# Cross-attention and soft mixture of experts on one core: Mu's norms spread through memory, and the second layer norm's first part on GpSimd

## The reference

```
x = x + cross_attention(layernorm(x), ctx, pos)     # 32 heads of 8, rotary positions
z = layernorm(x); x_ln = layernorm(z) * gamma + beta
mu_n = mu / |mu|  over the 256 rows, for each of 16 experts x 128 slots
logits = normalised(x_ln) * scale @ mu_n
dispatch = softmax over the 64 rows; combine = softmax over the 2048 slots
out = combine @ (gelu((dispatch.T @ x_ln) @ W1 + b1) @ W2 + b2)
x = x + out
```

## Time and profile before

| | us |
|---|---|
| median of 3 runs (lowest, highest) | 476.96 (475.56, 477.92) |
| the profiled execution, its span | 477.61, 475.7 |
| PE busy, PEld busy | 444.3, 382.1 |
| DVE, ACT, POOL busy | 389.0, 286.7, 182.8 |
| start until T_0 | 23.4 |
| attention steps, T_0 to T_15 | 153.4 |
| the rest | 298.9 |

### The profile page before, as it was taken

How to read it: one execution, slowest core, us unless ns; L and a number is a source line. 1 busy time by engine, 2 the same in 40 slices (tenths; PEclk the granted TensorE clock), 3 DMA queues, 4 the chain that set the end, 5 groups by cost and what they waited for, 6 DMA issues and landing times.

```text
span 475.7 us, 12795 instructions
## 1 busy us (share of the span) xinstructions
PE 444.3 (93%) x4816; PEld 382.1 (80%) x4816; DVE 389.0 (82%) x857; ACT 286.7 (60%) x553; POOL 182.8 (38%) x322
## 2 busy tenths in 40 slices
PE   0679999999999999999999999999999999999996
PEld 0557787878887778878888988988988988988985
DVE  6689888898889877977977977977977877887775
ACT  3457777778888666365466466457457447447443
POOL 4479998379996332114112112112112112202100
PEclk9979999999999799999999999999999999999999
DMA  8930000000003000223213223312312312312330
GB/s 231 271 152 23 3 3 23 1 4 1 3 1 72 3 2 1 52 56 83 68 52 84 68 55 77 77 50 72 83 50 66 88 50 61 99 44 55 99 92 22
DMA packets 27815, 28.54 MB, mean 60 GB/s; under 512 B 10960, under 2 KB 19072, under 8 KB 27520
## 3 DMA queue, kind: packets, MB, share of 16 engines
q1 hardware_dynamic: 27392, 27.48, 22.1%
q10 hardware_dynamic: 384, 0.52, 0.5%
HBM read 9.11 MB, written 2.10 MB: 24 GB/s over the span
## 4 chain that ended last, share of the span: by engine, by line
PE 74%; DVE 14%; POOL 4%; SPq 3%; DMA 2%; issue 2%; ACT 1%; ACTq 0%; DVEq 0%; POOLq 0%
PE bank L1025 13%; PE bank L1027 12%; PE bank L1026 12%; PE bank L1241 10%; PE bank L1121 6%; PE bank L1263 6%; PE bank L1104 3%; PE bank L1085 3%; PE bank L1142 2%; SPq L293 2%; DVE kT L758 2%; DMA xa<-in_x 2%; DVE pT L904 2%; DVE on L777 1%; DVE pb L932 1%
## 5 line engine op out<-in xcount | busy, mean ns | idle before, releaser
L904 DVE STREAM_TRANSPOSE pT<-eb 128x512 f32<-128x512 f32 x64 | 44.5, 700 | 38.3 <-ACT eb L618 35.0
L1241 PE MATMUL bank<-w_raw,eb 128*128 128x130 f32 x512 | 60.8, 276 | 1.3 <-DVE w_raw L895 1.3
L1241 PEld LDWEIGHTS bank<-w_raw,eb 128*128 128x128 f32 x512 | 58.5, 190 | 2.7 <-DVE w_raw L895 2.3
L629 ACT ACTIVATE pb<-pb 128x768 f32<-128x768 f32 (+1 forms) x48 | 37.2, 774 | 28.2 <-DVE pb L932 28.2
L1025 PE MATMUL bank<-mun_h,xlT_l 128*128 128x512 f32 x128 | 52.1, 407 | 0.0
L932 DVE TENSOR_TENSOR pb<-bank,rh 128x384 f32<-128x384 f32 x96 | 49.3, 513 | 3.3
L624 ACT CAST xlT_h<-bank 128x256 fp32r<-128x256 f32 x16 | 5.9, 372 | 76.1 <-PE bank L1213 76.1
L618 ACT ACTIVATE eb<-bank,nshift,rn 128x512 f32<-128x512 f32 x64 | 46.2, 776 | 7.8 <-PE bank L1027 7.6
L1027 PE MATMUL bank<-mun_h,xlT_h 128*128 128x512 f32 x128 | 50.5, 395 | 0.0
L545 ACT COPY pT<-bank 128x512 f32<-128x512 f32 x64 | 37.6, 588 | 21.3 <-PE bank L1104 20.5
L1026 PE MATMUL bank<-mun_l,xlT_h 128*128 128x512 f32 x128 | 50.5, 394 | 0.0
(11 more groups left out here) (159 smaller groups left out, 1155.4 us busy)
## 6 DMA issues: line engine op xcount, KB each, us to landing
mu_raw<-pT SPq DMA_DIRECT2D x248, 64.0 KB, 2.0
mu_raw<-in_L_ffn_mu SPq DMA_DIRECT2D x1, 2048.0 KB, 10.1
out<-w_raw SPq DMA_DIRECT2D x16, 128.0 KB, 1.9
xa<-in_x SPq DMA_DIRECT2D x1, 1536.0 KB, 8.5
w_raw<-in_L_ffn_W SPq DMA_DIRECT2D x2, 512.0 KB, 10.1
w_raw<-in_L_ffn_W SPq DMA_DIRECT2D x1, 1024.0 KB, 7.3
xa<-in_x SPq DMA_DIRECT2D x1, 512.0 KB, 3.5
ctile<-in_ctx SPq DMA_DIRECT2D x1, 512.0 KB, 5.2
```

The source lines that it names most:

```text
L904: v.transpose(eblk[:, :, 4 * c:4 * c + 4, :].rearrange("p m e j -> p e m j"), eb[:, 4 * c:4 * c + 4, :].rearrange("p e (m j) -> p e m j", ...
L1241: m = mm(bank[HB[i]][:, n * 2 * HC:(n + 1) * 2 * HC], eb[:, e, :], xw[:, e, :], start=True, stop=True)
```

## The change

Mu's norms no longer go through PE and ScalarE. Behind its context loads SP writes the 2048 norms as one row into memory, waits until it has landed, and loads the row into all 128 partitions of `mu_rb`. GpSimd waits for that once and scales Mu in steps 9 to 12. The eight instructions of the moments of tiles 0 to 10 move from VectorE's step 12 to GpSimd, behind its step 14, with the deviations behind them (these were behind step 13). The two centres move from VectorE's step 13 to GpSimd, each ahead of its affine. VectorE gets a wait for the deviations ahead of its first `ffn_step`.

```diff
 sync:      load_ctx(2, 12, 16)
+           sp.wait_ge(mur_ready, 1)
+           sp.dma_start(norm_row.rearrange("(e s) -> s e", s=SLOTS), mu_r[:, 1, :], ...).then_inc(row_loaded, 16)
+           sp.wait_ge(row_loaded, 16)
+           sp.dma_start(mu_rb, row(norm_row, ES)).then_inc(rb_loaded, 16)
 gpsimd:
+           def moments(t0, t1):      # the eight instructions of VectorE's moments, with its waits
+               ...
+           def center(t):
+               g.tensor_scalar(xl[:, t, :], xa[:, t, :], ln2[:, 4, t].unsqueeze(1), ln2[:, 6, t].unsqueeze(1),
+                               ALU.subtract, ALU.mult).then_inc(z_ready, 1)
 scale_mu:
-               if k == 0:
-                   pool.wait_ge(rb_ready, c + 1)
+               if c == 0 and k == 0:
+                   pool.wait_ge(rb_loaded, 16)
             step(7, (mu_norms, ()))
+            step(8)
             for c in range(NQ):
-                step(8 + c, (scale_mu, (c, 0)), (scale_mu, (c, 1)))
-            step(12)
+                step(9 + c, (scale_mu, (c, 0)), (scale_mu, (c, 1)))
             step(13)
-            pool.wait_ge(var_ready, 1)
+            step(14)
+            pool.wait_ge(st2_ready, TILES - LATE)
+            moments(0, TILES - LATE)
+            pool.wait_ge(zvar_step, 8)
             deviations(ln2, 0, TILES - LATE, r2_step, 0, r2_ready)
-            step(14)
+            pool.wait_ge(r2_ready, 1)
...
+            center(0)
             affine(0, 0)
+            center(1)
             affine(1, 1)
 scalar:
-            def rb_copy(c):
...
 vector:
-                if s == TILES - 4:
-                    dve.wait_ge(st2_ready, TILES - LATE)
-                    moments(st2, ln2, 0, TILES - LATE, 1 + LN_EPS, LN_EPS * LN_EPS, var_step, 0, var_ready)
-                if s == TILES - 3:
-                    dve.wait_ge(r2_ready, 1)
-                    center(0, 0)
-                    center(1, 1)
...
+            dve.wait_ge(r2_ready, 1)
             ffn_step(0, 0, first=True)
 tensor:
-            def spread_norms(c):
...
-                if 8 <= s < 8 + NQ:
-                    spread_norms(s - 8)
...
-                if 8 <= s < 8 + NQ:
-                    pe.wait_ge(rb_ready, s - 7)
```

More of the change, by code:

```diff
@@ L148, in build @@
         mur_ready = sem("mur_ready")
-        rb_filled = sem("rb_filled")
-        rb_ready = sem("rb_ready")
+        row_loaded = sem("row_loaded")
+        rb_loaded = sem("rb_loaded")
         muscale_step = sem("muscale_step")
@@ L199, in build @@
         z_ready = sem("z_ready")
+        zvar_step = sem("zvar_step")
         aff_step = sem("aff_step")
@@ L240, in build @@
         out_d = out.rearrange("b s d -> (b s) d").rearrange("(t p) d -> p t d", p=P)
+        norm_row = nc.dram_tensor("norm_row", (ES,), F32, kind="Internal").ap()
         def row(v, n):
@@ L315, in _ @@
             load_ctx(2, 12, 16)
+            sp.wait_ge(mur_ready, 1)
+            sp.dma_start(norm_row.rearrange("(e s) -> s e", s=SLOTS), mu_r[:, 1, :], allow_slow_non_contiguous=True)                .then_inc(row_loaded, 16)
+            sp.wait_ge(row_loaded, 16)
+            sp.dma_start(mu_rb, row(norm_row, ES)).then_inc(rb_loaded, 16)
             sp.wait_ge(mu_ready, NQ * KD)
@@ L385, in deviations @@
                     .then_inc(done, 1)
+            def moments(t0, t1):
+                L = [ln2[:, i, t0:t1] for i in range(8)]
+                st = [st2[:, t0:t1, i] for i in range(6)]
+                g.tensor_tensor(L[0], st[1], st[4], ALU.add).then_inc(zvar_step, 1)
+                g.tensor_tensor(L[1], st[1], st[4], ALU.subtract).then_inc(zvar_step, 1)
+                g.tensor_tensor(L[2], st[2], st[5], ALU.add).then_inc(zvar_step, 1)
+                pool.wait_ge(zvar_step, 3)
+                g.tensor_scalar(L[4], L[0], 0.5, None, ALU.mult).then_inc(zvar_step, 1)
+                g.tensor_tensor(L[3], L[1], L[1], ALU.mult).then_inc(zvar_step, 1)
+                pool.wait_ge(zvar_step, 5)
+                g.tensor_scalar(L[3], L[3], DIM / 4.0, None, ALU.mult).then_inc(zvar_step, 1)
+                pool.wait_ge(zvar_step, 6)
+                g.tensor_tensor(L[2], L[2], L[3], ALU.add).then_inc(zvar_step, 1)
+                pool.wait_ge(zvar_step, 7)
+                g.tensor_scalar(L[5], L[2], (1 + LN_EPS) / DIM, LN_EPS * LN_EPS, ALU.mult, ALU.add)\
+                    .then_inc(zvar_step, 1)
+            def center(t):
+                g.tensor_scalar(xl[:, t, :], xa[:, t, :], ln2[:, 4, t].unsqueeze(1), ln2[:, 6, t].unsqueeze(1),
+                                ALU.subtract, ALU.mult).then_inc(z_ready, 1)
             def split_pool(raw, halves, base, done):
@@ L513, in _ @@
                 if t == 0:
-                    pool.wait_ge(var_ready, 2)
+                    pool.wait_ge(var_ready, 1)
                     deviations(ln2, TILES - LATE, TILES, r2_step, 5, r2_ready)
@@ L576, in xT_high, with step @@
                 a.copy(flat(xT[0][:, t % 2]), bank[7][:, 0:3 * P]).then_inc(xT_split, 1)
-            def rb_copy(c):
-                act.wait_ge(rb_filled, c + 1)
-                a.copy(mu_rb[:, c * BANK:(c + 1) * BANK], bank[6][:]).then_inc(rb_ready, 1)
-            def step(s, norms=None):
+            def step(s):
                 if s >= 1:
                     pT_copy(s - 1, 3)
-                if norms is not None:
-                    rb_copy(norms)
                 exp_group(s, 0)
@@ L663, in _ @@
             for s in range(TILES):
-                step(s, s - 8 if 8 <= s < 8 + NQ else None)
+                step(s)
             act.wait_ge(shift_ready, 1)
@@ L1004, in _ @@
             stats(TILES - 1)
+            dve.wait_ge(r2_ready, 1)
             ffn_step(0, 0, first=True)
             dve.wait_ge(st2_ready, TILES)
-            moments(st2, ln2, TILES - LATE, TILES, 1 + LN_EPS, LN_EPS * LN_EPS, var_step, 7, var_ready)
+            moments(st2, ln2, TILES - LATE, TILES, 1 + LN_EPS, LN_EPS * LN_EPS, var_step, 0, var_ready)
             ffn_step(1, 1)
```

## The result

The changed kernel takes 477.91 us (475.90 to 480.08 in 20 runs) against 476.62 (474.94 to 478.24 in 20 runs): ratio 1.0029, interval 1.0016 to 1.0041. It is slower by 0.16 to 0.41 percent, where 472.0 was forecast.

The account below looks back on a forecast made before the run. PE, holding 74% of the chain, was taken to set the time. Terms 2.77 + 3.54 - 0.86 - 0.13 = 5.32 gave 472.3 against the profiled 477.61, 471.6 against the median; forecast 472.0, range 470.6 to 475.2.

Parts of the forecast that it names:

- The row through memory: Norms written, then broadcast, before GpSimd's step 9: 5.4 + 6.4 = 11.8 us of 14.15 allowed, no cost.
- the estimate beside it, 10.1: Row write by the skill's rule at W1's price: 10.1 + 6.4 = 16.5, GpSimd 2.35 late, time 474.4.
- the row is late: Rival: both transfers cost 10.1, PE waits 5.1 us in step 10, half clock follows: 480.5; chance 0.07.
- Spreading by PE goes: Steps 8 to 11: without the spreading matmuls they become plain steps of 9.49 us, a gain of 2.77.
- Moments and centres leave VectorE: Step 13 becomes a plain step if the half clock goes with the stall: a gain of 3.54 us.
- `scale_mu` one step later: GpSimd falls 0.6 us behind per scaling step; PE waits 0.27 in step 12, 0.59 in step 13: costs 0.86.
- the half clock stays: Rival: PE's 0.59 us wait in step 13 keeps the half clock; price 2.5, time 474.5; chance 0.22.
- Moments, deviations and centres on GpSimd: Behind `rope_sums(15)`: tile 0 ready at T_14 + 11.32, so PE waits 0.13 us.
- GpSimd is slower at the moments: Rival: moments at upper bound, tile 0 comes 2.8 us later, PE waits in step 15: 474.8; chance 0.06.
- The sum: Whole change: 2.77 + 3.54 - 0.86 - 0.13 = 5.32 us gained.

Follow-up runs that it names:

- the wide row: Changed kernel with the norms turned by a PE transpose and VectorE copy, written as 16 pieces of 512 bytes: 472.44 us, ratio 0.9917.
- the write alone: Kernel before with the write of 2048 norms as 4-byte pieces added, read by nobody, PE and ScalarE still spreading: 481.18 us, ratio 1.0102.
- the moments alone: Kernel before with only moments and first two centres moved to GpSimd, norms still spread by PE: 474.44 us, ratio 0.9976.
- Lighter steps: Kernel of the wide row with Mu's eight halves scaled 2, 2, 1, 2, 1 in steps 9 to 13: 471.21 us, ratio 0.9909.
- the row by slots: Changed kernel with the row written as 128 pieces of 64 bytes, GpSimd reading with a 64-byte step: 475.90 us, ratio 0.9986.
- the quarter of the row: Kernel before with 512 pieces of 4 bytes written side by side, read by nobody: 483.79 us in one execution.

## Why the prediction was wrong

**The step that failed is "The row through memory".** It took the row's landing from the positions (5.4 us) and W1 (10.1), and concluded "no cost". The row took 10.7, over the upper bound. That alone would hardly have hurt. The broadcast landed 4.7 us after its issue (the page's issue list), so both took 15.4 us. The 14.15 allowed were too few, because `add_bout` also stands ahead of the first scaling. In the wide row that scaling starts 4.61 us behind T_9, not 3.96, so 14.8 were allowed and with plain steps the two would have been 0.6 late:

```profile
122.42 1.27 POOL L467 TENSOR_TENSOR mu_raw<-mu_raw,eb 128x512 f32<-128x512 f32 x1
```

What was wrong is the frame: the step asked only when the row arrives, and who waits for it. Nobody waited for it in step 9, but PE, ScalarE and VectorE stood still while it settled, and PE came back at half clock. That is 4.95 us, and that the write of the small pieces causes it is shown from both sides: the write alone brings it into the kernel before (14.51 us in step 8), and leaving it out, making it wide, setting the pieces apart or sending them to SBUF takes it away. Both bounds were loads into SBUF; neither could show how small pieces side by side settle in memory.

The rival "the row is late" had the right transfer but another mechanism: it put the loss at PE's wait for a late GpSimd, in step 10, and there is none there (9.50 us).

The rule of the Trainium skill that the prediction weighed ("DMA: Bandwidth & Descriptors", section "Rules for kernel authors" and the specifications: one descriptor for each element, read-modify-write below 512 bytes) pointed at the right transfer. That the estimate beside it, 10.1, was close to 10.7 is luck: it is the price of W1, a load of 64 times as many bytes. Nor does size alone decide: pieces of the same 4 bytes landed in 4.1 us when they were 64 bytes apart.

**Spreading by PE goes:** right. Steps 9 to 12 take 9.50 us; step 8 would, as the wide row shows (9.49).

**Moments and centres leave VectorE:** the mechanism was right, the size was not. Step 13 fell to a plain step (9.50 with the moments alone), but the 3.54 us rested on one execution whose half clock lasted long. In most traces the same stall costs 11.5 - 9.5 = 2.0 us, and the timed gain of this part alone is 1.5. The term was too large by some 1.5 us.

**`scale_mu` one step later:** right, and a little dear. GpSimd's `rope_sums` starts behind T by 1.38, 1.91, 2.47 and 3.07 us in steps 10 to 13, on its timeline after, with PE's wait in step 13 below:

```profile
133.87 1.64 POOL L386 TENSOR_TENSOR qkr<-ra,rb 128x256 f32<-128x256 f32 x2
...
143.90 1.66 POOL L386 TENSOR_TENSOR qkr<-ra,rb 128x256 f32<-128x256 f32 x2
...
153.96 1.67 POOL L386 TENSOR_TENSOR qkr<-ra,rb 128x256 f32<-128x256 f32 x2
...
164.06 1.64 POOL L386 TENSOR_TENSOR qkr<-ra,rb 128x256 f32<-128x256 f32 x2
...
165.75 0.33 PE L1089 MATMUL bank<-ident,qkr 128*128 128x128 f32 x1 [0.37 <-POOL qkr L386]
```

The step grows by 0.25. Behind the standstill GpSimd starts step 9 earlier, 0.84 us behind T_9; in the wide row it starts 1.11 behind, and PE waits 0.16 us in step 12 and 0.70 in step 13:

```profile
160.90 0.33 PE L1096 MATMUL bank<-ident,qkr 128*128 128x128 f32 x1 [0.70 <-POOL qkr L389]
```

That is the 0.86 of the forecast, but the two steps grow by only 0.61. Lighter steps take it away. The rival "the half clock stays" didn't come true at these waits: the clock is 1.00 in both steps. It did in the row by slots, behind a wait of 1.19.

**Moments, deviations and centres on GpSimd:** right. On GpSimd's timeline the eight moments take 173.43 to 175.59, 2.16 us (2.3 forecast), and the deviations 3.35 (3.34):

```profile
173.43 0.23 POOL L400 TENSOR_TENSOR ln<-st 128x11 f32<-128x11 f32 x1
...
175.59 2.14 POOL L360 TENSOR_TENSOR ln<-ln,mhalf 128x11 f32<-128x11 f32 x1
...
178.73 0.21 POOL L369 TENSOR_TENSOR ln<-ln 128x11 f32<-128x11 f32 x1
179.04 1.24 POOL L416 TENSOR_SCALAR xl<-xa,ln 128x256 f32<-128x256 f32 x1
...
182.05 0.41 PE L1225 MATMUL bank<-ident,xl 128*128 128x128 f32 x2
```

PE took tile 0 at 182.05, T_14 + 11.32, 0.13 later than before. The rival "GpSimd is slower at the moments" fell.

**The sum:** by step times, 2.77 + 2.0 - 0.61 - 0.13 = 4.0 without the standstill; the wide row measures 475.94 - 472.44 = 3.5. In the changed kernel the lag costs 0.25 instead of 0.61, so with the standstill's 4.95 it is a loss of 0.6 us; 1.3 was measured. What is left, 0.7, stays open. The write alone leaves about as much: 481.18 - 475.94 = 5.2 against 4.3 in its step 8.

How a write that has left the DMA engines stops PE and ScalarE is not settled. No row shows what they waited for ("issue", "remote"). Records are missing there too. The row's semaphore counts to 16 as it lands. The traces hold 11 of these 16 signals after, 13 in the write alone and 1 in the quarter of the row, but all 16 in every trace where the row landed without a standstill. Every run here is a recorded one; whether it is instructions, semaphores or the records themselves that were held up, and whether it happens without recording, wasn't tried.

## What to carry to other kernels

A transfer of a few KB can cost more than its lateness: look in the trace at what all engines do between its last packet and its landing. Write a column of scalars to memory as few wide pieces (a transpose and a copy were free here), or set pieces of 4 bytes 64 bytes or more apart. And before a half-clock stretch goes into a sum, look at more than one execution: here the same stall cost 2.0 us in five traces and over 3 in two.

## What the runs showed of the hardware that was not expected

Pieces of 4 bytes from different partitions side by side in memory land 10.7 us after issue, as far as SP's next issue shows it, and 4.1 when each has 64 or 512 bytes for itself; into SBUF 3.0; 128 pieces of 64 bytes 2.1; 16 of 512 bytes 1.4. In the traces with the slow kind PE and ScalarE stop for 2 to 5 us, and VectorE with them, while GpSimd goes on; 512 such pieces do that no less than 2048 (17.07 us against 14.51 in step 8). GpSimd's multiplication of 512 columns takes 1.54 us instead of 1.28 when one operand is read with a step of 64 bytes.
